# Masks added by DMA, score rows fetched from DRAM lines, weights split one layer ahead

## What is computed

```python
mask = adj + eye > 0
for l in range(3):
    si = x @ attn_w[l, :d];  sj = x @ attn_w[l, d:]
    s = si[:, :, None] + sj[:, None, :] + attn_b[l]
    s = where(s >= 0, s, 0.2 * s);  s = where(mask, s, -inf)
    agg = softmax(s) @ x
    h = layernorm(x + agg, g1[l], beta1[l])
    x = layernorm(h + gelu(h @ W1[l] + b1[l]) @ W2[l] + b2[l], g2[l], beta2[l])
```

## Time and profile before

| | before |
|---|---|
| median of 3 runs (lowest to highest) | 2569.89 us (2567.87 to 2573.53) |
| profiled execution, time | 2566.34 us |
| its span, first to last instruction | 2564.5 us |
| PE, DVE, ACT, POOL busy in the span | 2390.6, 2295.8, 1791.0, 888.5 us |
| DMA, mean busy share of 16 engines | 34.5% (queue q1) |

### The profile page before, as it was taken

The page is one execution under the profiler, slowest core; times in us unless marked ns, Lnnn a source line. Parts: engine busy times, 40 slices in busy tenths (PEclk is TensorE's granted clock), DMA queues, the critical chain, the costliest instruction groups (busy, mean ns, idle before and its releaser), DMA issues.

```text
span 2564.5 us, 46231 instructions
## 1 busy us (share of the span) xinstructions
PE 2390.6 (93%) x16548; PEld 2188.5 (85%) x16548; DVE 2295.8 (90%) x5214; ACT 1791.0 (70%) x2873; POOL 888.5 (35%) x1125
## 2 busy tenths in 40 slices
PE   7999999993799999999989999999998999999996
PEld 6999999982688889888878889988888888988996
DVE  4888888886799999999989999999997999999885
ACT  3444444442688788788777887877877788787884
POOL 3555555553232231232213223213221443442321
PEclk9999999996799999999999999999998999999998
DMA  4444444435233233233233432323333243342321
GB/s 136 140 136 146 136 147 136 146 106 140 74 91 87 79 91 84 66 91 87 83 86 84 95 79 83 91 67 83 91 87 91 75 116 87 95 116 55 82 50 41
DMA packets 349877, 247.34 MB, mean 96 GB/s; under 512 B 214480, under 2 KB 308688, under 8 KB 349648
## 3 DMA queue, kind: packets, MB, share of 16 engines
q1 hardware_dynamic: 349648, 244.39, 34.5%
HBM read 143.68 MB, written 50.33 MB: 76 GB/s over the span
## 4 chain that ended last, share of the span: by engine, by line
PE 28%; DVE 27%; ACT 9%; issue 8%; POOL 4%; DMA 1%; SPq 1%; ACTq 0%; POOLq 0%; DVEq 0%
DVE spare L1143 4%; DVE g_lo L1253 4%; ACT t L1041 3%; DVE t L1154 3%; PE G L45 3%; PE G L43 3%; PE G L44 3%; PE Y L1466 3%; DVE t L1160 3%; ACT pT_hi L1040 3%; PE A L1415 3%; PE Y L1467 3%; PE Y L1468 3%; PE A L1416 2%; PE A L1417 2%
## 5 line engine op out<-in xcount | busy, mean ns | idle before, releaser
L1076 ACT ACTIVATE g<-G,b_less 128x512 f32<-128x512 f32 x384 | 264.8, 690 | 338.2 <-PE G L45 300.0
L1466 PE MATMUL Y<-w_hi,g_hi 128*128 128x256 f32 x1536 | 446.8, 291 | 57.9 <-DVE g_lo L1253 56.7
L1415 PE MATMUL A<-x_hi,pT_hi 128*128 128x258 f32 x1536 | 439.8, 286 | 24.0 <-DVE pT_lo L1166 21.2
L1416 PE MATMUL A<-x_hi,pT_lo 128*128 128x258 f32 x1536 | 436.9, 284 | 0.0
L1417 PE MATMUL A<-x_lo,pT_hi 128*128 128x256 f32 x1536 | 434.3, 283 | 0.0
L1467 PE MATMUL Y<-w_lo,g_hi 128*128 128x256 f32 x1536 | 428.5, 279 | 0.0
L1468 PE MATMUL Y<-w_hi,g_lo 128*128 128x256 f32 x1536 | 428.1, 279 | 0.0
L1466 PEld LDWEIGHTS Y<-w_hi,g_hi 128*128 128x128 f32 x1536 | 289.2, 188 | 99.0 <-DVE g_lo L1253 84.7
L977 POOL TENSOR_TENSOR ve<-mv,eps 128x4 f32<-128x4 f32 x48 | 29.1, 606 | 885.5 <-DVE mv L1200 885.5
L1415 PEld LDWEIGHTS A<-x_hi,pT_hi 128*128 128x128 f32 x1536 | 293.1, 191 | 35.1 <-issue 22.6
L43 PE MATMUL G<-h_hi,w_hi 128*128 128x512 f32 x768 | 307.6, 401 | 5.0 <-DVE h_lo L1248 4.5
(11 more groups left out here) (186 smaller groups left out, 6253.8 us busy)
## 6 DMA issues: line engine op xcount, KB each, us to landing
mask<-mask SPq DMA_DIRECT2D x192, 256.0 KB, 3.5
a_adj_t<-in_adj SPq DMA_DIRECT2D x64, 512.0 KB, 4.0
x_rows<-rows SPq DMA_DIRECT2D x24, 1024.0 KB, 7.4
mask<-a_mask SPq DMA_DIRECT2D x64, 256.0 KB, 4.3
rows<-xo SPq DMA_DIRECT2D x32, 512.0 KB, 2.9
a_xs<-in_x SPq DMA_DIRECT2D x9, 1024.0 KB, 9.4
x_rows<-in_x SPq DMA_DIRECT2D x8, 1024.0 KB, 7.6
rows<-a_xo SPq DMA_DIRECT2D x64, 128.0 KB, 3.7
```

The costliest lines, as they stand in the source:

```text
L1415: pe.matmul(L.A[:, t, 0:DE], hi, L.x_hi[:, par, j, :], start=(j == 0), stop=False)
L1416: pe.matmul(L.A[:, t, 0:DE], lo, L.x_hi[:, par, j, :], start=False, stop=False)
L1466: pe.matmul(L.Y[:, t, :], hi, L.w2[0][:, f, :], start=False, stop=False)
```

## The change

Four things are changed, all in `graph_layers`.

- VectorE's `add_mask` is gone. GpSimd issues instead four DMAs for each chunk (`add_masks`), each of which adds two mask tiles (bf16, SBUF) onto two tiles of t (float32, SBUF). ScalarE's exps wait for them, and so does SP's next `load_maskT`.
- From batch 2 on, the rows don't go through TensorE and ScalarE. SP stores the columns to DRAM lines (`store_v`, `store_r`: elements of 4 bytes) and loads them back onto all partitions (`load_v`, `load_r`). Batches 0 and 1 keep the old way.
- Layer 0's weights are split as before. Those of layers 1 and 2 are loaded, split and stored to DRAM (512 KB for each f) in turns 4 to 11 of the layer before, one f in a turn, and loaded complete by `load_split` at the new layer's first chunk.
- VectorE's queue is written anew: two row_tops ahead of sums, two in the f loop at 6 and 7; scaled in the loop at f = 2 and 3; stats1 behind f = 1; score one f earlier (SCORED); projections at 4 to 7; the last layer's steps at 4, 5 and 7. SP's queue is rearranged to match.

The core of the diff:

```diff
-    L.w1 = [sb("w1_hi", [P, KD, F], F32R), sb("w1_lo", [P, KD, F], F32R)]
-    L.w2 = [sb("w2_hi", [P, KF, D], F32R), sb("w2_lo", [P, KF, D], F32R)]
+    L.w = sb("w", [P, KF, 4, D], F32R)
...
+    SCORED = ((0, 1), (2,), (3,), (4,), (5,), (6,), (7,), ())
...
+    def w1_part(part, f, i):
+
+        return L.w[:, f, 1 - part, i * P:(i + 1) * P]
+
+    def w2_part(part, f):
+
+        return L.w[:, f, 3 - part, :]
+
+    def split_at(k):
+
+        f = k % C - 4
+        return [f] if layer_of(k) < LAYERS - 1 and 0 <= f < KF else []
...
             def load_maskT(k, half):
                 if k > 0:
-                    sp.wait_ge(L.s_tm, NT * (k - 1) + HALF * (half + 1))
+                    for g in range(2 * half, 2 * half + 2):
+                        sp.wait_ge(L.s_tm[g], 16 * k)
...
+            def store_v(n):
+                slot = NCH * n % C
+                if n >= B:
+                    sp.wait_ge(L.s_uv, 2 * TC * (NCH * n + NCH - C))
+                with nc.allow_non_contiguous_dma("a column to a line"):
+                    for c in range(NCH):
+                        sp.dma_start(vline[n, c * BANK:(c + 1) * BANK].rearrange("(t p) -> p t", p=P),
+                                     L.uv[:, slot + c, 1, :]).then_inc(L.s_vline, 16)
+
+            def load_v(n):
+                sp.wait_ge(L.s_vline, 32 * (n - 1))
+                sp.wait_ge(L.s_top, NT * (n - 1))
+                sp.dma_start(L.vrow[:, n % 2, :], vline[n].partition_broadcast(P)).then_inc(L.s_vrow_in[n % 2], 16)
+
+            def store_r(n):
+                sp.wait_ge(L.s_cols, COLS * (n + 1))
+                with nc.allow_non_contiguous_dma("two columns to lines"):
+                    for part in range(2):
+                        sp.dma_start(rline[n, part].rearrange("(s p) -> p s", p=P), L.rcol[:, part, :]).then_inc(L.s_rline, 16)
+
+            def load_r(k):
+                n, cs = k // 2, slice(k % 2 * BANK, (k % 2 + 1) * BANK)
+                sp.wait_ge(L.s_rline, 32 * n)
+                sp.wait_ge(L.s_t, NT * (k - 1))
+                for part in range(2):
+                    sp.dma_start(L.rrow[:, part, k % 2, :], rline[n, part, cs].partition_broadcast(P)).then_inc(L.s_rrow_in[k % 2], 16)
...
+            def load_raw(layer, f):
+                n = KF * (layer - 1) + f
+                if n == 0:
+                    sp.wait_ge(L.s_w_lo, KF)
+                else:
+                    sp.wait_ge(L.s_split_out, 16 * n)
+                raw_weights(layer, f, 0, L.s_raw_in)
+
+            def store_split(layer, f):
+                sp.wait_ge(L.s_raw_lo, KF * (layer - 1) + f + 1)
+                sp.dma_start(split[layer - 1, f], L.x1[:, :, :]).then_inc(L.s_split_out, 16)
+
+            def load_split(layer, f):
+                if f == 0:
+                    sp.wait_ge(L.s_split_out, 16 * KF * layer)
+                sp.wait_ge(L.s_ffn2, KF * (C * layer - 1) + f + 1)
+                sp.dma_start(L.w[:, f, :, :].bitcast(F32), split[layer - 1, f]).then_inc(L.s_split_in, 16)
...
                 if k % 2 == 0 and k < K - 2:
                     load_x(k // 2 + 1)
+                if k % 2 == 1 and (k + 7) // 2 < NB:
+                    store_v((k + 7) // 2)
+                if k % 2 == 1 and k + 2 < K:
+                    load_r(k + 2)
+                for n in rows_made(k):
+                    load_v(n)
                 if 2 <= k and layer_of(k - 2) == LAYERS - 1:
                     load_x1(k - 2)
-                for r in tops[:1]:
+                for f in split_at(k):
+                    load_raw(layer_of(k) + 1, f)
+                for r in tops[:2]:
                     load_mask(r + MASKS)
-                if k >= 2:
+                arriving = layer_of(k) if k < K and new_layer(k) else 0
+                if k == 0:
+                    for f in range(2, KF):
+                        first_weights(f)
+                if arriving:
+                    for f in range(3):
+                        load_split(arriving, f)
+                if k >= 2 and layer_of(k - 2) < LAYERS - 1:
                     store(k - 2)
-                if k < K and new_layer(k):
-                    for f in range(2 if k == 0 else 0, KF):
-                        load_weights(layer_of(k), f)
+                if k % 2 == 0 and k + 2 < K:
+                    store_r((k + 2) // 2)
                 if k + 2 < K:
-                    for half in range(2):
-                        load_maskT(k + 2, half)
-                for r in tops[1:]:
+                    load_maskT(k + 2, 0)
+                if k % 2 == 0 and k + 2 < K:
+                    load_r(k + 2)
+                for f in split_at(k):
+                    store_split(layer_of(k) + 1, f)
+                if arriving:
+                    for f in range(3, KF - 3):
+                        load_split(arriving, f)
+                for r in tops[2:]:
                     load_mask(r + MASKS)
+                if k + 2 < K:
+                    load_maskT(k + 2, 1)
+                if arriving:
+                    for f in range(KF - 3, KF):
+                        load_split(arriving, f)
+                if k >= 2 and layer_of(k - 2) == LAYERS - 1:
+                    store(k - 2)
...
+            def add_masks(k, groups):
+                for g in groups:
+                    pool.wait_ge(L.s_t, NT * k + 2 * g + 2)
+                    pool.wait_ge(L.s_maskT[g // 2], 16 * (k + 1))
+                    pool.dma_start(L.t[:, 2 * g:2 * g + 2, :], L.maskT[:, 2 * g:2 * g + 2, :], accum_op=ALU.add).then_inc(L.s_tm[g], 16)
+
...
                 for n in rows_made(k):
                     v_prepare(n)
+                if k + 1 < K:
+                    add_masks(k + 1, range(1))
                 if k < K:
                     deviation1(k)
+                if k + 1 < K:
+                    add_masks(k + 1, range(1, 3))
                 if k - 2 >= K - C:
                     deviation3(k - 2 - (K - C))
+                if k + 1 < K:
+                    add_masks(k + 1, range(3, 4))
...
-                act.wait_ge(L.s_tm, n + 1)
+                act.wait_ge(L.s_tm[j // 2], 16 * (k + 1))
...
+            def raw_hi(layer, f):
+                n = KF * (layer - 1) + f
+                act.wait_ge(L.s_raw_in, 32 * (n + 1))
+                act.activation(L.x1[:, 1:4:2, :].bitcast(F32R), L.x1[:, 0:4:2, :], ACT.Copy).then_inc(L.s_raw_hi, 1)
...
-                    if f == 3:
-                        for n in rows_made(k):
-                            copy_v(n)
-                    if f == 4 and k + 2 < K:
-                        for part in range(2):
-                            copy_rows(k + 2, part)
                     if f in (5, 6) and k < K:
                         for t in (0, 1) if f == 5 else (2, 3):
                             n1(k, t)
...
+                    if f == 1 and k < K:
+                        for i in split_at(k):
+                            raw_hi(layer_of(k) + 1, i)
...
-
-            def add_mask(k, j):
-                dve.wait_ge(L.s_t, NT * k + j + 1)
-                dve.wait_ge(L.s_maskT[j // HALF], 16 * (k + 1))
-                dve.tensor_tensor(L.t[:, j, :], L.t[:, j, :], L.maskT[:, j, :], ALU.add).then_inc(L.s_tm, 1)
...
+            def raw_lo(layer, f):
+                dve.wait_ge(L.s_raw_hi, KF * (layer - 1) + f + 1)
+                dve.tensor_tensor(L.x1[:, 0:4:2, :].bitcast(F32R), L.x1[:, 0:4:2, :], L.x1[:, 1:4:2, :],
+                                  ALU.subtract).then_inc(L.s_raw_lo, 1)
...
                 if agg:
-                    p_lo(k, LEAD)
+                    for j in range(LEAD, LEAD + 2):
+                        p_lo(k, j)
                 if old:
                     stats2(k - 2)
                 if agg:
-                    for j in range(LEAD + 1, NT):
+                    for j in range(LEAD + 2, NT - 1):
                         p_lo(k, j)
                 if k == 0:
                     for r in range(NT, NT + NT - 1):
                         row_top(r)
-                for r in tops[:min(early, 2)]:
+                for r in tops[:1]:
                     row_top(r)
+                if agg:
+                    p_lo(k, NT - 1)
                 if ffn:
                     h_lo(k - 1)
-                for r in tops[2:early]:
-                    row_top(r)
-                if old:
-                    scaled(k - 2)
                 if ffn and new_layer(k - 1):
                     less_b2(layer_of(k - 1))
+                if k >= 1:
+                    for r in tops[1:2]:
+                        row_top(r)
                 if agg:
                     sums(k)
                 for f in range(KF):
                     if ffn:
                         g_lo(k - 1, f)
-                    if f == 0 and agg:
+                    if f == 1 and agg:
                         stats1(k)
-                    if f in (1, 3, 5, 6) and projected:
-                        projections(k - 2, ((f + 1) // 2 - (f < 6),))
```

(53 more changed lines are left out.)

144 lines of the change are left out of this document (79 added, 65 removed).

## The result

The changed kernel takes 2621.9 us (2620.6 to 2631.7), the kernel before in the same runs 2568.9 us: a ratio of 1.021, 95% interval 1.018 to 1.024. It is slower by 53 us where 120 us less were forecast. The profiled execution of it has a span of 2621.0 us.

A forecast was written before the change was run, and what follows sets the result against it. VectorE sets the pace, TensorE just behind (floor 35.92 of 38.57 us a chunk). Regular chunks -61, last layer -22.7, boundaries -34, first two steps -3: together -121 from span 2564.5, so 2449 us; range 2415 to 2590.

The forecast's parts named there:

- Rows: Rows through DRAM lines: TensorE loses 1.5 us per chunk; the new transfers cost 0, DMA engines about 4 us more.
- Weights: Splitting leaves the layer boundaries: two steps take 78.3 us; 16 turns with a split get one VectorE subtraction, 0.6 us.
- Masks: Mask adds leave VectorE, 4.8 us less per chunk; each DMA add 5 us (2.9 to 9.3), path cost 0.
- the forecast's own signs of being wrong: Exponentials waiting for `t<-maskT`, DMA share above 0.8, scores or row_tops waiting for DMAs, GpSimd's issues delaying n1 or n2.
- late by about 1.3: VectorE in the last layer: final_sum, final_stats, final_norm replace projections, 1.3 us more, so 37.2 us a chunk.
- VectorE's order: VectorE's f loop goes from 21.65 to 20.4 us, late by 0 to 0.6, taken as 0.5: 36.4 us a chunk.
- rival A: TensorE at its floor, no lateness of VectorE: 2420 us; chance 0.11.
- Boundaries: Two layer boundaries fall from 93.6 and 97.1 to 78.3 us each, -34 in all; split loads 0, at most +4 each.
- group 3: A chunk's last mask add (j = 6, 7): about 9 us from score to need, against 5 for the DMA.
- Start: First chunk: adds after GpSimd's columns start ScalarE 1 to 3 us later, seven row_tops cover it: 0 to +2.
- B: New waits in SP's or GpSimd's in-order queue make a turn late by another 1.2 us: 2498 us; chance 0.14.
- C: DMA engines become the bound; adds occupy them A us each, meeting 36.4 at A = 5.1; 6.5 gives 2728; chance 0.23.

The follow-up runs named there:

- the best version: Changed kernel with rows on TensorE and two repairs: first chunk's masks by VectorE, last three split loads ahead of `load_maskT(k + 2, 1)`; 2472.7 us, 0.962.
- the kernel with masks and order alone: Changed kernel with rows on TensorE and weights split at each layer's first chunk; masks by DMA and VectorE's new order stay; 2521.4 us, 0.982.

## Why the prediction was wrong

The forecast was 2449 us, the result 2621.9. Each term of the sum, for the changed kernel and for the one with larger pieces, in which only the pieces of the column stores are different (differences to the span of before, us):

| term | forecast | changed kernel | with larger pieces |
|---|---|---|---|
| start and first chunk | 0 to +2 | +9.3 | +7.9 |
| first two steps | -3 | -4.7 | -2.9 |
| 28 turns | -61 | +64.9 | -73.3 |
| two boundaries | -34 | +4.3 | -15.5 |
| last layer | -22.7 | -22.3 | -25.3 |
| tail | 0 | +4.9 | +3.2 |
| sum | -121 | +56.5 | -105.9 |

**The failed step** is in Rows: "SP issues two stores of 1024 elements of 4 bytes for a batch (4.0 KB in such elements land in 3.1 us" and after it "Cost 0; the DMA engines get about 4 us more for each chunk". The count was wrong: a batch has 3072 pieces in four stores (v's 1024 in two, r's 2048 in two). The price was wrong too. The 3.1 us of the earlier trace rows is the median landing of three loads of columns, read without a look at what stands behind them. In the changed kernel v's first stores stand ahead of these same three loads, and they take 9.1 us:

```profile
b<-in_L_gnn_b SPq DMA_DIRECT2D x3, 4.0 KB, 9.1
```

In the loop v's stores stand in SP's queue ahead of rrow, vrow and the raw weights, and vrow lands in 13.3 us, against 6.8 when only v's pieces are larger. A landing time was read as a cost to the stores' user; what counted was what stands behind them. The trace of before had the sign in it. While SP issued such columns of 4-byte elements, the DMA engines were a third busy at 3 GB/s (columns as in the earlier trace rows, GB/s last):

```profile
602.00:604.00 2.00, 0.00 (x0) 0.00 (x0) 1.93 (x4) 1.40 (x3) 0.00 (x0) 0.50 0.32 3
```

The Trainium skill has the rule on the pieces ("DMA: Bandwidth & Descriptors", Rules for kernel authors): a strided last dimension becomes one descriptor per element, and should be rearranged to be contiguous. The packet counts of this case agree to the piece.

**Weights**, the second failed step: the staging was costed as "one subtraction of 128x512", 0.6 us of VectorE. ScalarE's raw_hi and its wait for the load were never costed, nor who stands behind it: g_hi, g_lo, TensorE. This is where the late load became 15.5 us of everybody's time, in 8 turns, those with v's store ahead. The loss needs both failures: without staging 97 us come back, with the load moved ahead 98, without the row lines 136, with larger pieces 160. They overlap and can't be added.

**Masks** held where the row lines were out of the way. Against "I take 5 us", the add lands in 4.5 to 4.8 us in the three kernels with rows on TensorE, in 7.4 in the changed one, where ScalarE's exponentials wait 33.7 us for it, one of the forecast's own signs of being wrong; with larger pieces that wait is 2.4 us in all. By the Trainium skill ("DMA: Bandwidth & Descriptors", Anatomy of one DMA: 2.0 us plus bytes by 436 GB/s) an estimate is 3.2 us (the bytes written) to 5.0 (all bytes): the traces lie in between, near the upper. Of the rule of the Trainium skill ("SBUF — State Buffer", Who interferes with whom) that a DMA issued by GpSimd can wait while VectorE runs in a two-port mode, no run shows a sign: what made the adds late went with the row lines. The last layer gained the forecast 22 us, with "late by about 1.3" in it.

**VectorE's order** held: turns of 35.9 us on average with larger pieces, "36.4 us for a chunk, between 35.9 ... and 37.3" forecast. The 35.9 is rival A's number, TensorE's floor of 35.92: the 0.5 us that VectorE was to be late doesn't show, and the 28 turns gain 73.3 us where 61 were forecast. With rows on TensorE they are 36.8, so taking the transposes off is worth 0.9 us for a chunk.

**Boundaries** were mis-sized: 88.4 and 86.8 us with larger pieces, 81.2 and 81.1 in the best version, against 78.3. "0, at most +4 for each boundary" for the split loads was too little while they stand behind the wait for group 3: TensorE waits for them 28 us in the changed kernel, 14 with larger pieces. In the best version no such wait is left among those of 640 us and later. **Start**: "0 to +2" was +9.3; the first adds come after GpSimd's columns, and the seven row_tops that were to cover this did not.

**Rivals.** B was the direction, with a wrong place and size: not "another 1.2 us" in every turn but 10 us in every second staged one. C is refuted with its A: queue 0's share is 20.5% of 2621.0 us for 192 adds, 2.8 us each (2.2 with rows on TensorE), far below 5.1, and without any add on the DMA engines vrow landed as late. Its sign, a DMA share near 0.8, did appear (0.79 and 0.80 in the regular stages), but the kernel with larger pieces moves the same bytes with 0.71 and 0.73 at TensorE's floor. The range ended at 2590, 32 us short: it left out most of C and gave B, which has a wait in order that could be any length, only 49 us.

## What to carry to other kernels

Count a transfer in pieces, not only in bytes, and ask what stands behind it in its queue: a slice in which the DMA engines are a third busy at a few GB/s, while loads are outstanding, is the place to look first. Where an engine gets a new instruction in the middle of its queue, cost its wait for the worst landing of what it reads, and give it a place where nothing waits behind it, or issue its load first. Replacing a 512 KB load by another changed nothing; changing the access pattern of stores of 2 and 4 KB changed 160 us.

## What the runs showed of the hardware

- Stores in 4-byte pieces: 58112 pieces more cost 46.5% x 2621.0 - 43.4% x 2458.6 = 152 us of all 16 engines, an estimated 42 ns of one engine for a piece. v's pieces alone (46.3% of 2545.3 us, 16896 pieces fewer) give 38 ns, the rest 43. It is more likely too high than too low, since the other transfers of the queue can have been slowed too. In one slice behind such a store the DMA moved 8 GB/s.
- An accumulating DMA of 512 KB float32 += bfloat16 in SBUF lands in 4.5 to 4.8 us, occupies all engines for about 2.2 us, and takes GpSimd 0.97 us to issue (mean of 192).
- VectorE reads of float32 in SBUF with 16 bytes between the starts of neighbours (both row inputs): score takes 1146 ns in place of 743; with 32 bytes (vrow), row_top takes 2109 in place of 1220. The Trainium skill ("SBUF — State Buffer", Door 1: The DMA port swizzle) has four float32 as how far one can stride for free; here that costs 54%. The shape of the access changes with it (4 x 128 in place of 512), and the two weren't measured apart.
- A broadcast of one 4 KB line of DRAM to 128 partitions lands no later than 512 KB from 128 places (13.3 and 14.1 us behind the same stores; 6.3 us behind larger pieces).

Open are why SP took 7.13 us to issue the raw load (1.00 us in the same turn with v's pieces larger), the long boundaries of the kernel with masks and order alone, the 3 to 5 us of the tail, and rows through DRAM in the right order without small pieces, by one transpose of the columns on TensorE before the store: it was not tried. The kernel with larger pieces, whose numbers are not the reference's, is 11 us under the best version and still lacks its 18 us at the start and the boundaries (5.6 + 7.1 + 5.7). So a kernel with rows in the right order and both repairs would, by an estimate that leaves out the cost of that transpose, be 11 to 29 us under 2472.7.
